# Loading the first experts' weights in quarters between a slot stage and an expert stage

## What is computed

```
q = broadcast(slot_query)                       # [8, 16, 512]
o = q + mha(q, x, x, d_Wq, ..., d_Wo, d_bo)     # the slot stage
h = layernorm(o) * e_ln_g + e_ln_b              # one row of gain and shift for each expert
u = silu(einsum('besd,edf->besf', h, e_W1) + e_b1)
g = silu(einsum('besd,edf->besf', h, e_Wg) + e_bg)
y = einsum('besf,efd->besd', u * g, e_W2) + e_b2
out = mha(x, o + y, o + y, c_Wq, ..., c_Wo)     # the last stage
```

## Time and profile before

| | us |
|---|---|
| median of 3 runs | 2421.1 |
| the runs | 2413.06 to 2422.67 |
| the profiled execution | 2415.6 |
| its span, from the first to the last instruction | 2413.8 |
| slot loop, batches 1 to 7 | about 1686 to 1787 |
| end of the slot stage | about 1788 to 1817 |
| expert stage | about 1817 to 2270 |
| last stage | about 2270 to 2414 |

### The profile page before, as it was taken

How to read it: one execution, slowest core, us unless ns; L and a number is a source line. 1 busy time by engine, 2 the same in 40 slices (tenths; PEclk the granted TensorE clock), 3 DMA queues, 4 the chain that set the end, 5 groups by cost and what they waited for, 6 DMA issues and landing times. The chain is left out here.

```text
span 2413.8 us, 30028 instructions
## 1 busy us (share of the span) xinstructions
PE 2131.5 (88%) x11425; PEld 1592.4 (66%) x11425; DVE 1335.3 (55%) x2112; ACT 673.0 (28%) x1066; POOL 618.8 (26%) x552
## 2 busy tenths in 40 slices
PE   6999999999989999999999999998997527445898
PEld 5677777776767778888888888887873102111477
DVE  7665665556447777666766676666651000000377
ACT  2544564446533321212111212222420000000231
POOL 5444654355348850320032000000320000000010
PEclk9999999999999999999999999998997768677999
DMA  4223223311287659664966494434769999999857
GB/s 155 76 102 128 75 72 111 128 62 62 88 319 298 239 209 377 227 217 160 358 223 221 158 369 161 161 128 151 297 269 410 426 430 426 427 429 428 302 227 261
DMA packets 181397, 565.13 MB, mean 234 GB/s; under 512 B 15473, under 2 KB 98961, under 8 KB 152561
## 3 DMA queue, kind: packets, MB, share of 16 engines
q1 hardware_dynamic: 171952, 504.37, 55.4%
q10 hardware_dynamic: 9312, 58.99, 5.9%
HBM read 450.07 MB, written 113.25 MB: 233 GB/s over the span
## 5 line engine op out<-in xcount | busy, mean ns | idle before, releaser
L1446 PE MATMUL ff_down<-w,u 128*128 128x512 f32 x1536 | 360.8, 393 | 11.4 <-DVE ff_x L1720 10.2
L1386 PE MATMUL ff_up<-ff_t,w 128*128 128x512 f32 x1488 | 357.6, 389 | 0.0
L1446 PEld LDWEIGHTS ff_down<-w,u 128*128 128x128 f32 x1536 | 288.2, 189 | 78.0 <-DVE ff_x L1720 17.2
L1386 PEld LDWEIGHTS ff_up<-ff_t,w 128*128 128x128 f32 x1488 | 279.6, 188 | 58.1
L1720 DVE SCALAR_TENSOR_TENSOR ff_x<-ff_down,gates,ff_x 128x512 f32<-128x512 f32 x256 | 190.8, 748 | 85.5 <-PE ff_down L1446 83.6
L2474 PE MATMUL e_down<-e_w,e_ug 128*32 128x512 f32 x480 | 77.2, 802 | 180.9 <-DMA e_w<-in_L_ffn_e_W 180.9
L1386 PE MATMUL ff_up<-ff_b,w 128*128 128x512 f32 x960 | 235.8, 389 | 0.0
L1386 PEld LDWEIGHTS ff_up<-ff_b,w 128*128 128x128 f32 x960 | 180.2, 188 | 37.4
L2474 PEld LDWEIGHTS e_down<-e_w,e_ug 128*32 128x32 f32 x480 | 17.8, 142 | 239.0 <-DMA e_w<-in_L_ffn_e_W 190.7
L2576 DVE TENSOR_TENSOR e_u_rows<-e_turned,e_b1T 128x128 f32<-128x128 f32 x16 | 4.7, 291 | 264.6 <-PE e_turned L2465 264.6
L1511 ACT ACTIVATE ff_gate<-ff_gate 128x512 f32<-128x512 f32 x62 | 39.2, 633 | 400.2 <-DVE ff_gate L1696 400.2
(11 more groups left out here) (449 smaller groups left out, 4400.5 us busy)
## 6 DMA issues: line engine op xcount, KB each, us to landing
w<-ff_w_factors SPq DMA_DIRECT2D x48, 1792.0 KB, 7.4
e_w<-in_L_ffn_e_W SPq DMA_DIRECT2D x17, 4096.0 KB, 22.1
e_wg<-in_L_ffn_e_Wg SPq DMA_DIRECT2D x16, 4096.0 KB, 30.0
e_w<-in_L_ffn_e_W ACTq DMA_DIRECT2D x13, 4096.0 KB, 51.4
ff_w_factors<-w SPq DMA_DIRECT2D x15, 1792.0 KB, 7.0
w<-ff_w_parts SPq DMA_DIRECT2D x48, 512.0 KB, 5.7
ff_t<-ff_t_factors SPq DMA_DIRECT2D x16, 1024.0 KB, 13.9
ff_b<-xnT SPq DMA_DIRECT2D x11, 1024.0 KB, 11.0
```

The costliest lines, as they stand in the source:

```text
L1386: last = nc.tensor.matmul(bank[:, :], a, m, start=start and c == 0, stop=stop and c == 5)
L1446: last = nc.tensor.matmul(DN[m % 2][:, :], a, w, start=c == 0, stop=c == 5)
```

## The change

It does four things.

- Expert 0's twelve quarters of 1 MiB are sent one by one, each as soon as the tile under it has been read for the last time: a quarter of W1 in the loop at b = 1 (over `wkT`), another at b = 6 (over `y_xin`), the others between the last scores and the end of the values. Expert 1's Wg and a quarter of its W1 are sent while the end of the slot stage runs, and two more quarters at the head of the expert stage; the last quarter waits for the turned biases.
- The 26 small row loads (`b2`, `bo_rows`, and eight each of three kinds) become five, with one broadcast DMA for each of the three kinds, and stand at b = 1 and b = 2.
- The bias rows lie in the last quarter of expert 1's W1 rather than in its Wg, and are sent during the end of the slot stage.
- PE turns the biases between `e_u` and `e_g` of expert 0 instead of behind `e_g`.

```diff
@@ sync of the slot stage
+                if b == B - 2:
+                    sp.wait_ge(y_ready, B)
+                    load_w1_part(sp, first_w1, I["L0_ffn_e_W1"][0], 3, w1_in[0])
                 if b + 1 < B:
                     keep(b + 1)
                 if b < 4:
                     load_w2_part(sp, second_w2, I["L0_ffn_e_W2"][1], b, w2_in[1])
-                if b == 5:
+                if b == 1:
+                    sp.wait_ge(built, BUILT[f"A{CH - 1}"])
+                    load_w1_part(sp, first_w1, I["L0_ffn_e_W1"][0], 1, w1_in[0])
                     sp.dma_start(b2[:, :], I["L0_ffn_e_b2"]).then_inc(gains_in, 16)
                     sp.dma_start(bo_rows[:, :], I["L0_ffn_d_bo"].unsqueeze(0).to_broadcast([P, D])).then_inc(gains_in, 16)
-                    for n in range(B):
-                        sp.dma_start(o1[n * NS:(n + 1) * NS, :], I["L0_ffn_slot_query"].rearrange("o s d -> (o s) d")).then_inc(gains_in, 16)
-                if b == 6:
-                    for n in range(B):
-                        sp.dma_start(e_gain[n * NS:(n + 1) * NS, :], I["L0_ffn_e_ln_g"]).then_inc(gains_in, 16)
-                        sp.dma_start(e_shift[n * NS:(n + 1) * NS, :], I["L0_ffn_e_ln_b"]).then_inc(gains_in, 16)
-            sp.wait_ge(yn_lo_done, B)
+                if b == 2:
+                    for to, name in ((o1, "slot_query"), (e_gain, "e_ln_g"), (e_shift, "e_ln_b")):
+                        rows = I[f"L0_ffn_{name}"]
+                        rows = rows if name == "slot_query" else rows.unsqueeze(0)
+                        sp.dma_start(to[:, :], rows.to_broadcast([B, NS, D])).then_inc(gains_in, 16)
             sp.wait_ge(scored, B * 2)
-            load_w1(sp, first_w1, I["L0_ffn_e_W1"][0], w1_in[0])
-            sp.wait_ge(g_ready, done("z", B - 1, 1))
-            load_w1(sp, first_wg, I["L0_ffn_e_Wg"][0], wg_in[0])
+            load_w1_part(sp, first_w1, I["L0_ffn_e_W1"][0], 0, w1_in[0])
             for part in range(2):
                 sp.wait_ge(yT_out[part], B * 16)
+                load_w2_part(sp, first_w2, I["L0_ffn_e_W2"][0], part, w2_in[0])
+            sp.wait_ge(yn_lo_done, B)
+            load_w1_part(sp, first_w1, I["L0_ffn_e_W1"][0], 2, w1_in[0])
+            sp.wait_ge(g_ready, done("z", B - 2, 1))
+            for k in (0, 2):
+                load_w1_part(sp, first_wg, I["L0_ffn_e_Wg"][0], k, wg_in[0])
+            for n, rows in enumerate(bias_rows):
+                sp.dma_start(rows, I["L0_ffn_e_" + ("b1", "bg")[n]]).then_inc(bias_in, 16)
+            sp.wait_ge(g_ready, done("z", B - 1, 1))
+            for k in (1, 3):
+                load_w1_part(sp, first_wg, I["L0_ffn_e_Wg"][0], k, wg_in[0])
+            load_w2_part(sp, first_w2, I["L0_ffn_e_W2"][0], 2, w2_in[0])
             sp.wait_ge(g_ready, len(order))
-            load_w2(sp, first_w2, I["L0_ffn_e_W2"][0], w2_in[0])
+            load_w2_part(sp, first_w2, I["L0_ffn_e_W2"][0], 3, w2_in[0])
+            sp.wait_ge(built, BUILT["slots_out"])
+            load_w1(sp, second_wg, I["L0_ffn_e_Wg"][1], wg_in[1])
+            load_w1_part(sp, second_w1, I["L0_ffn_e_W1"][1], 0, w1_in[1])
@@ a new function
+def load_w1_part(queue, w1, src, k, arrival):
+    queue.dma_start(w1[:, k, :], src.rearrange("(p k) n -> p k n", k=KT)[:, k, :]).then_inc(arrival, 16)
@@ sync of the expert stage
-                for i, n in enumerate(("b1", "bg")):
-                    sp.dma_start(bias_rows[i], I[f"L0_ffn_e_{n}"]).then_inc(bias_in, 16)
-                load_w1(sp, w1[1], I["L0_ffn_e_W1"][1], w1_in[1])
+                for k in (1, 2):
+                    load_w1_part(sp, w1[1], I["L0_ffn_e_W1"][1], k, w1_in[1])
                 sp.wait_ge(bias_turned, 2)
-                load_w1(sp, wg[1], I["L0_ffn_e_Wg"][1], wg_in[1])
+                load_w1_part(sp, w1[1], I["L0_ffn_e_W1"][1], 3, w1_in[1])
@@ tensor of the expert stage, grow and start
                         last.then_inc(ready, 1)
+                        if between and ready is u_ready:
+                            between()
...
+                def turn_bias():
                     pe.wait_ge(bias_in, 32)
                     for n in range(2):
                         for f, at in enumerate(block_at):
-                            last = nc.tensor.transpose(TB[n][:, f * E:(f + 1) * E], bias_rows[n][:, at], ident[0:E, 0:E])
+                            last = nc.tensor.transpose(TB[n][:, f * E:(f + 1) * E], bias_rows[n][:, at], ident[32 * n:32 * n + E, 32 * n:32 * n + E])
                         last.then_inc(bias_turned, 1)
+
+                def start(e, i):
+                    grow(e, i, turn_bias)
                     pe.wait_ge(bias_ready, 2)
                     turn(e)
```

More of the change, by code:

```diff
@@ L1819, in slot_attention @@
             over.sbuf("values_out_weights_place", [P, 2, KT, D])
+            over.sbuf("second_w1_first_part", [P, D])
             e_gain, e_shift, h_in, o1 = (over.sbuf(n, [P, D]) for n in ("e_gain", "e_shift", "h_in", "o1"))
@@ L1823, in slot_attention @@
             bo_rows = over.sbuf("bo_rows", [P, D])
+        with ExitStack() as plan:
+            plan.enter_context(nc.sbuf_tensor("to_second_w1", [P, (low_bytes - 4 * KT * FF) // 4 - B * TT * 6], F32))
+            second_w1 = plan.enter_context(nc.sbuf_tensor("e_w1_1", [P, KT, FF], F32))
+        bias_rows = [second_w1[32 * n:32 * n + E, KT - 1, :] for n in range(2)]
         mem.sbuf("slot_weights_place", [P, 4, KT, D])
@@ L1849, in slot_attention @@
         z = mem.sbuf("z", [P, 2, D])
+        with nc.sbuf_tensor("e_wg_1", [P, KT, FF], F32) as second_wg:
+            pass
         zT = mem.sbuf("zT", [P, KT, SH, B, NS])
@@ L2336, in expert_low_bytes, with experts @@
     return 4 * (2 * FT * E + KT * 32 + 2 * FF // 4 + FT * 32 + D + B + KT * FF) + 224
-def experts(nc, whole, I, ident, hT, o2T, early_w, w1_in, wg_in, w2_in):
+def experts(nc, whole, I, ident, hT, o2T, early_w, w1_in, wg_in, w2_in, bias_rows, bias_in):
     with ExitStack() as stage:
@@ L2375, in experts @@
         w1, wg, w2 = [w1_0, w1_1], [wg_0, wg_1], [w2_0, w2_1]
-        bias_rows = [wg[1][0:E, i, :] for i in range(2)]
         UP = [mem.bank(f"e_{n}") for n in "ug"]
@@ L2380, in experts @@
         WB = [UP[0], UP[1], mem.bank("e_wq_turned0"), mem.bank("e_wq_turned1")]
-        bias_in, bias_turned, bias_ready, fold_ready = (mem.sem(f"e_{n}") for n in ("bias_in", "bias_turned", "bias_ready", "fold_ready"))
+        bias_turned, bias_ready, fold_ready = (mem.sem(f"e_{n}") for n in ("bias_turned", "bias_ready", "fold_ready"))
         h_ready, u_ready, g_ready, u_taken, g_taken, turned, pre_ready, silu_ready, ug_ready = (
@@ L2448, in _, with grow @@
             def _(pe):
-                def grow(e, i):
+                def grow(e, i, between=None):
                     pe.wait_ge(h_ready, e + 1)
-                    for bank, w, arrival, taken, ready in ((UP[0], w1[i], w1_in[i], u_taken, u_ready), (UP[1], wg[i], wg_in[i], g_taken, g_ready)):
-                        pe.wait_ge(arrival, arrived(e, i))
+                    for bank, w, arrival, value, taken, ready in ((UP[0], w1[i], w1_in[i], in_parts(e, i), u_taken, u_ready),
+                                                                  (UP[1], wg[i], wg_in[i], arrived(e, i) + 48 * (1 - i), g_taken, g_ready)):
+                        pe.wait_ge(arrival, value)
                         pe.wait_ge(taken, e)
@@ L2489, in both @@
                     add_parts(e)
-                def start(e, i):
-                    grow(e, i)
+                def turn_bias():
                     pe.wait_ge(bias_in, 32)
@@ L3069, in gated_block @@
                 ff, x1_stored, ff_down = feed_forward(nc, whole, taken, I, gates, first, turned_place, x_stats, load_slot, x1_begun, x1_d, xnT_d, t_d, made_pieces)
[L3070 removed]
+                early_w, w1_in, wg_in, w2_in, bias_rows, bias_in = slot_attention(nc, whole, I, ident, x_stats, slot_w, slot_w_in, slot_wo_in, slot_x, slot_x_in, slot_vectors, slot_small_in,
                                                               ff, x1_stored, ff_down, expert_low_bytes(), o2T, hT, x1_d, xnT_d)
[L3072 removed]
+            early_weights = experts(nc, whole, I, ident, hT, o2T, early_w, w1_in, wg_in, w2_in, bias_rows, bias_in)
         token_attention(nc, whole, I, ident, gates, 4 * KT * E * B + expert_low_bytes(), early_weights, o2T, bo_place, x1_d, xnT_d, out)
```

24 lines of the change are left out of this document (11 added, 13 removed).

## The result

The changed kernel takes 2409.85 us (median of 20 runs, 2403.5 to 2415.08) where the kernel before, run beside it, takes 2419.2 (20 runs, 2413.06 to 2424.96): a ratio of 0.9961, 95% interval 0.9953 to 0.9970, so 9.4 us faster, 7.3 to 11.4. That is inside the half per cent called "no change" above. The profiled execution took 2403.5 us, its span 2401.7, against 2415.6 and 2413.8. It is the fastest of the 20, so its own gain of 12.1 us is more than the change brings on average.

The account below looks back on a forecast made before the run. The expert stage was taken as bound by the transfer of 12 MiB an expert. 3 MiB fewer left (7.35 us) and a wait ending sooner (3.1 us) sum to 10.4: 2421.1 - 10.4 = 2410.7 us, range 2402 to 2418.

Parts of the forecast that it names:

- the half per cent called "no change" above: Whole kernel's time: about 0.5% (12.1 us) is what a measurement can tell from no change; chance of landing within it 0.63.

## What to carry to other kernels

Where a stage is bound by its bytes, count only the time in which the DMA engines have nothing to do, and take each edit for worthless until its pause would otherwise be the last one: two edits here were worth 3 us each beside the rest of the change, and 1 and 0 alone. Ask also which load PE waits for last and how much work stands behind it: with all W1 and Wg in quarters the last Wg landed together with W2, and the stage ended some 13 us later than the lower rate explains.
